# Moving the token products, the input split, the stack loads and a scaling in the slot plan of an attention and expert layer

## What is computed

```python
x = concatenate([input[:, o:o + 744] for o in (0, 3, 6)], axis=-1)
h = einsum('btd,od->bto', x, W) + b                # the token product
h = h + attention(layernorm(h))                    # 16 heads of 16, causal, 744 rows
h = h + experts(layernorm(h))                      # the best 2 of 4 experts, 256 -> 1024 -> 256, exact gelu
```

## Time and profile before

| | |
|---|---|
| median of 3 runs | 1868.71 us (1864.55 to 1869.48) |
| the profiled execution's own time | 1868.96 us |
| span from its first to its last instruction | 1867.2 us |
| mean granted TensorE clock | 0.901 of full |
| busy: PE, PEld, DVE, ACT, POOL | 1551.3, 1196.2, 1097.4, 709.6, 835.7 us |
| front, to the first exponential | 0 to 129.1 us |
| eight batches | 129.1 to 1159.5 us |
| tail and experts | 1159.5 to 1867 us |

### The profile page before, as it was taken

How to read it: one execution, slowest core, us unless ns; L and a number is a source line. 1 busy time by engine, 2 the same in 40 slices (tenths; PEclk the granted TensorE clock), 3 DMA queues, 4 the chain that set the end, 5 groups by cost and what they waited for, 6 DMA issues and landing times.

```text
span 1867.2 us, 33109 instructions
## 1 busy us (share of the span) xinstructions
PE 1551.3 (83%) x10648; PEld 1196.2 (64%) x10648; DVE 1097.4 (59%) x3458; ACT 709.6 (38%) x1463; POOL 835.7 (45%) x912
## 2 busy tenths in 40 slices
PE   2679798798798698698797787459999999999997
PEld 2536474474374374374464442459999999999997
DVE  1366668667577577577577580335555555555554
ACT  0114544444444444444434554023333333333332
POOL 4313334544634535536436335224444444545444
PEclk9759998898897798899898896779999999999999
DMA  3251633733724624625526457354545555554551
GB/s 93 70 108 41 169 85 103 194 85 99 193 63 127 164 73 138 150 68 155 137 69 170 104 163 214 96 169 157 198 163 186 181 177 184 169 197 152 192 175 62
DMA packets 166971, 256.23 MB, mean 137 GB/s; under 512 B 30484, under 2 KB 97998, under 8 KB 166800
## 3 DMA queue, kind: packets, MB, share of 16 engines
q1 hardware_dynamic: 108816, 166.66, 31.2%
q10 hardware_dynamic: 34368, 50.33, 9.1%
q0 software_dynamic: 23616, 37.12, 6.7%
HBM read 173.92 MB, written 75.29 MB: 133 GB/s over the span
## 4 chain that ended last, share of the span: by engine, by line
PE 53%; issue 14%; DVE 10%; DMA 9%; POOL 8%; ACT 3%; SPq 2%; ACTq 0%; DVEq 0%; POOLq 0%
PE yb L1383 14%; PE l1b L1370 13%; PE pab L1094 8%; PE pvb L1194 6%; DMA qk_s<-parts 5%; PE mxb L1154 4%; PE stb L1171 4%; POOL xs L674 4%; DVE unused L898 2%; PE rb L1341 1%; DMA r_s<-invs 1%; POOL prob L685 1%; DMA invb<-r_s 1%; PE pab L1136 1%; ACT hf L1254 1%
## 5 line engine op out<-in xcount | busy, mean ns | idle before, releaser
L760 ACT ACTIVATE prob<-stb 124x496 f32<-124x496 f32 (+2 forms) x832 | 401.7, 505 | 464.2 <-PE stb L1171 426.9
L898 DVE CUSTOM_DVE_ANT_0 unused<-mxb,mask_row 124x372 bf16<-124x372 f32 (+4 forms) x768 | 352.7, 484 | 84.9 <-PE mxb L1154 80.8
L1154 PE MATMUL mxb<-kst,qst 96*124 96x372 bf16 (+4 forms) x1024 | 321.2, 345 | 80.7 <-DVE mxp L898 47.8
L1171 PE MATMUL stb<-qst,kst 99*124 99x372 bf16 (+4 forms) x1024 | 316.9, 344 | 65.2 <-DMA qst<-negp 42.7
L1383 PE MATMUL yb<-w2p,hp 128*128 x2448 | 339.4, 284 | 10.1 <-DVE yo L1325 10.1
L1370 PE MATMUL l1b<-x2T,w1s 128*128 128x384 f32 x1632 | 336.5, 341 | 1.2 <-DVE x2T L1284 1.2
L1383 PEld LDWEIGHTS yb<-w2p,hp 128*128 128x128 f32 x2448 | 323.7, 189 | 20.5 <-issue 20.5
L1254 ACT ACTIVATE hf<-l1b,b1c 128x384 f32<-128x384 f32 x272 | 158.3, 582 | 340.5 <-PE l1b L1370 301.6
L1370 PEld LDWEIGHTS l1b<-x2T,w1s 128*128 128x128 f32 x1632 | 275.4, 189 | 1.6 <-DVE x2T L1284 1.6
L1171 PEld LDWEIGHTS stb<-qst,kst 99*124 99x124 bf16 x1024 | 138.8, 145 | 197.7 <-ACT prob L760 79.7
L1154 PEld LDWEIGHTS mxb<-kst,qst 96*124 96x124 bf16 x1024 | 141.3, 146 | 177.9 <-DVE mxp L898 94.8
(11 more groups left out here) (158 smaller groups left out, 1543.8 us busy)
## 6 DMA issues: line engine op xcount, KB each, us to landing
w1s<-ws SPq DMA_DIRECT2D x34, 2048.0 KB, 8.4
qk_s<-parts SPq DMA_DIRECT2D x64, 279.0 KB
xg<-xs SPq DMA_DIRECT2D x34, 396.0 KB
kst<-qk_s SPq DMA_DIRECT2D x32, 279.0 KB, 3.8
qst<-qk_s SPq DMA_DIRECT2D x32, 279.0 KB, 6.4
wraw<-in_w_all ACTq DMA_DIRECT2D x32, 256.0 KB
ws<-whi ACTq DMA_DIRECT2D x32, 256.0 KB
ws<-wlo ACTq DMA_DIRECT2D x32, 256.0 KB
```

The lines of the kernel that those rows point to most:

```text
L760: act.activation(dst, src, ACT.Exp, scale=DH ** -0.5).then_inc(exp_done, 1)
L898: done = dve.tensor_tensor_reduce(out=unused[:, n % 2, e * w:(e + 1) * w], in0=src, in1=mask_row[:, T - w:T], scale=1.0, scalar=-3.0e38, o ...
L1154: done = nc.tensor.matmul(out, qst[g % NG][0:ROWS, h + e, TT * i:TT * i + TT], kst[g % NG][0:ROWS, h + e, k0:k0 + w], start=True, stop=True)
L1171: done = nc.tensor.matmul(out, kst[g][:, h, TT * j:TT * j + TT], qst[g][:, h, q0:q0 + w], start=True, stop=True)
```

## The change

The plan alone changes, with one new kind of index: `x` events now have the pair (0 or 1, step), where 1 means the batch after the one that the body prepares.

- The input split moves from slots 2 to 8 of the next body into the end of this one, slots 90, 93, 96 and 99; `x_load` moves from slot 97 to 80. The front also splits the second batch's input, after `h1_store`.
- The token products move from slots 11, 13, ... 21 to 0, 2, ... 10; `norm`, `xn`, `turn`, `bias` and `h1_store` move up with them, to slots 12 to 29.
- q and k move from slots 38 to 68 up to 26 to 50. The stack loads move from 51, 72, 83 to 39, 57, 80.
- The first pair's scaling moves from slot 90 to slot 1 of the next body (`scale`, -2), and for the last batch to the tail.
- The steps of routing, scatters, weight splits, a fold and `h2_store` move by 1 to 4 slots, and the weight splits' third load from 47 to 50.

```diff
     for i in range(NT):
         put(5 + i, "v", i)
         if not last:
-            put(11 + 2 * i, "tok", i)
+            put(2 * i, "tok", i)
     if not first:
+        put(1, "scale", -2)
...
-        for i, s in enumerate((39, 40, 42, 43, 45, 46)):
+        for i, s in enumerate((38, 39, 42, 43, 45, 46)):
             put(s, "scale2", i)
-        put(41, "h2_store", 0)
-        for p, s in enumerate((48, 49, 51, 52)):
+        put(43, "h2_store", 0)
+        for p, s in enumerate((48, 49, 51, 53)):
             put(s, "gate", p)
-        put(54, "count", 0)
-        put(55, "place", 0)
-        put(56, "place", 1)
-        for i, s in enumerate((58, 61, 64, 67, 71, 74, 78, 81, 84, 88, 91, 95)):
+        put(56, "count", 0)
+        put(57, "place", 0)
+        put(58, "place", 1)
+        for i, s in enumerate((60, 63, 66, 69, 72, 75, 79, 82, 86, 89, 92, 95)):
             put(s, "scatter", i)
-    for g, s in ((0, 45), (1, 60), (2, 86)):
+    for g, s in ((0, 45), (1, 61), (2, 87)):
         put(s, "fold", g)
-    put(79, "spread_in", 0)
-    put(90, "scale", 0)
-    for n, (load, split, store) in enumerate(((2, 11, 17), (22, 28, 34), (47, 57, 63), (66, 76, 85))):
+    put(78, "spread_in", 0)
+    for n, (load, split, store) in enumerate(((2, 12, 17), (22, 32, 36), (50, 58, 64), (67, 77, 88))):
...
     if not last:
-        for p in range(2 * KC):
-            put(2 + 2 * p, "x", p)
-        put(22, "norm", 0)
+        put(12, "norm", 0)
         for i in range(NT):
-            put(24 + 2 * i, "xn", i)
-        for n, s in enumerate((30, 32, 35, 36)):
+            put(14 + i, "xn", i)
+        for n, s in enumerate((17, 18, 21, 22)):
             put(s, "turn", n)
-        for p, s in enumerate((35, 36, 37)):
+        for p, s in enumerate((21, 22, 24)):
             put(s, "bias", p)
-        put(53, "h1_store", 0)
+        put(29, "h1_store", 0)
         for n in range(4):
-            put(38 + 3 * n, "qk", n)
-            put(59 + 3 * n, "qk", n + 4)
-        put(51, "load_stack", 0)
-        put(72, "load_stack", 1)
-        put(83, "load_stack", 2)
-        put(97, "x_load", 1)
+            put(26 + 3 * n, "qk", n)
+            put(41 + 3 * n, "qk", n + 4)
+        put(39, "load_stack", 0)
+        put(57, "load_stack", 1)
+        put(80, "load_stack", 2)
+        put(80, "x_load", 1)
+        for p, s in enumerate((90, 93, 96, 99)):
+            put(s, "x", (1, p))
```

More of the change, by code:

```diff
@@ L88, in front_events @@
     for p in range(2 * KC):
-        yield "x", p
+        yield "x", (0, p)
     for i in range(NT):
@@ L100, in front_events @@
     yield "h1_store", 0
+    for p in range(2 * KC):
+        yield "x", (1, p)
     for m in range(KC):
@@ L221, in tail_events @@
             yield event
+    yield "scale", -2
     yield "fold", -1
@@ L640, in emit @@
                 for kind, n in events:
[L641 to L647, removed]
+                    if kind == "x" and a + n[0] < NB:
+                        at, p = a + n[0], n[1]
+                        c, step = divmod(p, 2)
+                        if p == 0:
+                            pool.wait_ge(x_loaded, (at + 1) * (16 * KC))
+                            if at:
+                                pool.wait_ge(tok_full, at * NT)
                         if step == 0:
@@ L650, in emit @@
                         else:
-                            pool.wait_ge(x_top, a * KC + c + 1)
+                            pool.wait_ge(x_top, at * KC + c + 1)
                             pool.tensor_tensor(xp[1][:, c, :], xraw[:, c, :], xp[0][:, c, :].bitcast(fp32),
```

## The result

| | before | after |
|---|---|---|
| median of 4 runs each | 1869.1 us (1864.55 to 1871.65) | 1936.84 us (1925.41 to 1938.13) |
| ratio | | 1.0352 (95% interval 1.0307 to 1.0396) |
| profiled execution, its span | 1868.96, 1867.2 us | 1938.13, 1936.4 us |
| mean granted TensorE clock | 0.901 | 0.886 |

Slower, as forecast, but by 68 us where the forecast had 9, and 22 us above the range. First the page of after: the busy times, and the clock over the span. TensorE is busy 31 us longer with the same 10648 products, at a lower granted clock (0.886 for 0.901); the other 38 of the span's 69 us are idle.

What follows compares the result with a forecast made beforehand. No engine bounds a batch; TensorE's work plus a few waits does. Six batches at +2.2 (+13), batch 7 -4 and front +0.5 add 9.5 to 1868.96, giving 1878 us, range 1816 to 1915.

Steps and rivals of the forecast that it cites:

- Slots 0 to 10 and 23 to 34: Six token groups enter the first, 10.5 to 23.5 us; three q/k groups enter the second as normalising leaves, 14.1 to 16.
- Slots 73 to 103: End of a batch: slot 78's wait goes, but the late input holds GpSimd's masks and slot 98; 38.7 to 37.7 us.
- One stack load leaves that time, one stays; I take 23: Residual's load from slot 73: 23 us assumed, between 28 at the lower packet rate and 12 at the higher.
- The 6 us in which slot 78 waited for the maxima's DMA go: Slot 78's wait disappears because that DMA no longer stands behind q/k group 7 on SyncE; 6 us.
- Slots 35 to 56: Five q/k groups come in, 24.4 us, plus 6 for a new store wait and lower clock: 30.4, before 33.6.
- A wait of 4: Near slot 50, ScalarE's eviction of group 7 waits for group 4's store, queued behind six stack loads; range 0 to 14.5.
- Slots 11 to 22: Token groups leave; normalising, subtractions and statistics fill VectorE: 15 us, before 20.2.
- Slots 57 to 72: Four q/k groups leave, so the stretch takes batch 7's 13.3 us, before 16.6.
- Batch 7: The last batch has none of the moved work and loses GpSimd's wait for the reciprocals: -4 us.
- both waits are longer: Rival, slower still: residual at 28 us and the slot 50 wait at 8, +8 a batch, 1925 us; chance 0.15.
- The input lands in time: Rival, faster: residual takes 12 to 17 us, so slots 73 to 103 take about 28; 1820 us; chance 0.20.
- the store does not wait: Rival, faster: group stores land early, so the 6 us at slot 50 go in seven batches; 1838 us; chance 0.12.

Runs made afterwards that it cites:

- the runs that take one wait away: The changed kernel with only the input's load moved from slot 80 to 62, 1887.93 us; or only the first stack load from 39 to 51, 1902.54 us.
- both out: The changed kernel with the input's load at slot 62 and the first stack load at slot 51: 1857.34 us, 0.9922 of the kernel before.

## Why the forecast was right in sign and wrong in size

The forecast's change of a batch against the measured one (means of batches 1 to 5; the stretches of before are 10.7, 20.2, 14.2, 34.2, 17.0 and 38.3, of after 23.0, 17.0, 15.9, 33.4, 15.4 and 41.1):

| slots | forecast | measured |
|---|---|---|
| 0 to 10 | +13.0 | +12.3 |
| 11 to 22 | -5.2 | -3.2 |
| 23 to 34 | +1.9 | +1.7 |
| 35 to 56 | -3.2 | -0.8 |
| 57 to 72 | -3.3 | -1.6 |
| 73 to 103 | -1.0 | +2.8 |
| sum | +2.2 | +11.4 (+11.2 by rounded rows) |

Five batches with 9.2 more each are 46 of the 60 us missed; batch 0 (+5.2 for 0), batch 7 (+3.8 for -4), front and tail (+2.2 for 0.5) and batch 6 (+1.1 for +2.2) make the rest.

- **Slots 0 to 10 and 23 to 34: right** within 0.7. Six token groups of 2.17 with nothing beside them, as the sum had it.
- **Slots 73 to 103: the mechanism was right, the landing mis-sized.** The wait at slot 98 came, behind the cast and the mask, as told. But the input landed 30.8 us after slot 73, not 26. "One stack load leaves that time, one stays; I take 23" was the failing step: the residual's last packet came 27.6 us after slot 73 began (29.3 in before), nearly the 28 of the lower rate that the forecast had as a bound. "The input's 750 KB need 3 more" held. In after ScalarE's queue moved 352 packets in 8.7 us, 40 a us; then the stack load and the broadcast came on top, and a run without that stack load got 37 us back. The higher of the two rates, 62 packets a us, was misread as well: the earlier trace rows have 889 packets and 1.02 MB for an output store of 744 packets and 0.76 MB, so the rest was the weights', and the store had 52 a us. From the landing to slot 104 the forecast had 10.2; here it was 983.6 - 973.7 = 9.9. "The 6 us in which slot 78 waited for the maxima's DMA go" was wrong too: some 3.5 of them stayed, and cost nothing here, since the input landed later still.
- **Slots 35 to 56: the wait was told, its size not.** "A wait of 4" was 7.4 in batch 5. Group 7 was ready 17.2 us after slot 35, as told (17 to 18); the stack's loads began at 10.4 (told: 9.5), and group 4's store landed 14.2 us after that (told: 12). The six loads cost SyncE 7.0 us (904.16 to 911.11), where the forecast took 2.7, and the small store then needed another 7.2. (Of the 14.5 us in the earlier trace rows only 8.7 lie behind the issue at 94.00.) The maxima's DMA landed with the store, as told, but had no cost of its own in the sum; it is what TensorE waited for. The run with the load at slot 51 got 5.0 us a batch back.
  The Trainium skill's rule that the prediction set against this (DMA: Bandwidth & Descriptors, Queues, rings and completion order), by which a later DMA may complete before an earlier one, did not show here: in batch 5 the six loads had landed by 916.2, the store behind them at 918.3.
- **Slots 11 to 22:** 17.0 for 15. VectorE is nearly full, as told. Two small operations of the maxima (24 x 124) took 2.6 us together while GpSimd ran the second pair's scaling, at slot 20 as before, and the biases, which moved up beside it; elsewhere in the batch the same operations take 0.2 and 0.3. VectorE's timeline of after:
```profile
871.39 1.31 DVE L923 CAST negp<-negr 24x124 bf16<-24x124 f32 x1
872.73 1.27 DVE L925 TENSOR_TENSOR negp<-negr,negp 24x124 bf16<-24x124 f32 x1
```
GpSimd's timeline at the same time:
```profile
870.87 1.76 POOL L693 TENSOR_TENSOR spare<-spare,invb 128x744 f32<-128x744 f32 x1
872.59 2.56 POOL L668 TENSOR_TENSOR h<-h,bp_row 124x520 f32<-124x520 f32 x2
```
  Each of the two ends just behind a GpSimd operation (872.63, and 873.9 for the first of the two biases), by 0.15 us at most, and so it is in every batch in which one is slow. That would be the 2.0 missed against batch 7, where neither is. No run took the overlap away, and in batches 1 to 6 of before the first of the two was slow too (1.5 us), so this share was only argued.
- **Slots 57 to 72:** 15.4 for 13.3. The clock was 0.78 there in batch 5, and 0.97 in the earlier trace rows. It is not the wait at slot 50 alone: without it the stretch still took 14.8. What else keeps the clock low stays open.
- **Batch 7:** the forecast gave it the whole of GpSimd's wait for the reciprocals. It went, and TensorE waited for the maxima's DMA instead, 8.9 us in this batch (1.1 before). Batch 7 was taken from a row of a wait, with no look at what came second; the run with the scaling alone shows the same for the other batches.

The rival that came nearest is "both waits are longer", at 1925. "The input lands in time" and "the store does not wait" did not come, but they priced the waits about right: 58 and 40 us, where the runs that take one wait away got 49 and 34 back. With both out the change is 1857, hardly less than the 1861 of the scaling alone. The time is lost in slots 0 to 34, 55.6 us a batch there and 45.2 with the scaling alone, and it is the token products that came into slots 0 to 10, with nothing beside them. With the transfers split, 49 us are lost by all that moved except q, k and the stack loads, and some 20 of them won back by these. How the 49 divide between token products, normalising, split and routing was not tried; the stretches put them in slots 0 to 10.

That the sign was right was in part luck: the forecast lay only 9 us over no change, its terms of either sign nearly cancelled, and it gave all slower cases together a chance of 0.44. Of the 60 us missed, some 31 came from the two landings of DMAs that it had too early (3.8 and 2.4 us in each of five batches).

## What to carry to other kernels

Before a step is moved towards the end of a stage, look at what is still in flight on its queue and how fast that goes: here a transfer of 744 packets at 30 to 40 a us decided the whole change, and splitting its 124 rows into 112 and 12 was worth more than any plan tried here. A wait that stands in the profile is worth only its distance to the next wait behind it: 8 us of waiting gave 1.4. And work that shares a stretch with another engine's is nearly free there, and costs its full time elsewhere: slots 0 to 10, which the six token groups entered, grew by 12.3 us; slots 11 to 22, which they left and the normalising entered, shrank by 3.2.

## What was not expected of the hardware

- A transfer of 124 rows was slow by its row count. The residual moved 257 (before) and 352 packets (after) in the first 8.7 us, and all of its 744 in 8 us as 112 and 12 rows. The kernel before gains 3.4% by splitting three such transfers.
- Issuing a DMA can block a compute engine: 13.3 us of ScalarE for one issue, while 924 packets of the input and the residual were still to move on its queue. The same issue took 0.35 us in after, with 320 left.
- Six issues of SyncE took 7.0 us at slot 39 and 3.9 at slot 80 (951.15 to 955.05).
- Small VectorE operations took 4 to 6 times their usual time (1.31 and 1.27 us for 0.21 and 0.28) while GpSimd multiplied and added whole tiles, and ended when its operation did.
- One scatter of GpSimd in the changed plan's batch 4 stood idle for 5.9 to 12.0 us, for a reason that the profile does not show.
